# A graph network on one core: layer 0 uses six more one-hot matrices, and the attribute product is done in four 64 by 64 tiles

## The chip, the cores and the metric

The kernel runs on one core of a Trainium2 chip. The metric is device time in microseconds (us) of one execution, as the median of several. A core has TensorE (matmul into PSUM), VectorE, ScalarE, GpSimd and SyncE, which run their instructions in order and wait for each other by semaphores, and DMA engines for transfers. In the profile PE is a TensorE matmul, PEld a weight load, DVE is VectorE, ACT is ScalarE, POOL is GpSimd, SP is SyncE; SPq, ACTq and so on are their DMA queues.

## The reference

A graph has 3125 nodes with 64 features and 103125 directed edges with 64 features, sorted by their target `dst`. Each of four layers does

```
msg   = relu(h[src] + e) + 1e-7        # e = edge_attr @ enc_edge_w + enc_edge_b, the same in all layers
m     = msg * t
ex    = exp(m - max of m over the edges of dst)
agg   = sum over the edges of dst of msg * ex / sum of ex
z     = relu(layernorm((h + agg) @ w1 + b1)) @ w2 + b2
```

with `h = x @ enc_node_w + enc_node_b` at first, and layer norms and residuals between the layers. All is float32.

## The kernel before

**Streams and chunks.** The sorted edges are cut into two halves. Half 0 lies on partitions 0 to 63 and half 1, reversed, on partitions 64 to 127, one feature to a partition and one edge to a column: 51712 columns, in 49 chunks of 1024 and a tail of 512, 512, 256, 128 and 128. Each layer goes over the 54 chunks, with running maxima and sums over the columns (scans on VectorE) in place of segment operations.

**One chunk c.** TensorE makes `x = h[src] + e` in one of four PSUM buffers `X` (two banks of 512 columns each):
- `edge_product` multiplies the attributes (`attr`, 128 rows: both halves' features) by `enc_edge2`, a block-diagonal 128 by 128 matrix with `enc_edge_w` twice, one matmul to a bank (L533). It waits for the buffer: `num_ready` of chunk c-4, VectorE's last scan of it (L956).
- `add_rows` adds `h[src]`: GpSimd gathers 128 rows of the table `z_table` at a time (L492, 16 gathers for a full chunk, 8 for each half), and TensorE adds them by transposes (L562). There are three gather buffers.
- For the `CHOSEN` chunks the second bank is not gathered (8 gathers less): `add_by_one_hot` adds `h[src]` by 150 matmuls with a one-hot matrix of 3200 node rows by 2 x 512 columns (L552), split into 25 blocks by three bf16 parts of the table by two halves. A matmul has all 128 rows and 64 output columns; halves 0 and 1 go in turn to PSUM partitions 0 to 63 and 64 to 127. Pieces 0 and 1 are part 0 (60 matmuls), pieces 2 to 4 are part 1 (90).

Then ScalarE applies the relu and t (L669, L671), VectorE runs the maximum (L925) and subtracts (L930), ScalarE takes exponentials (L681 to L686), VectorE sums (L940, L943, L956) and turns the sums (L911), and SyncE stores them (L362). ScalarE also makes penalties at segment starts from `keep` bytes that SyncE loads from DRAM (L352, L659).

**The one-hot matrices.** In layer 0 VectorE builds 31 of them, for the chunks in `BANKS`: chunks 0 and 1, the even ones from 4 to 48, and 5, 13, 21, 29, 37, 45. Each has five pieces (L1020), built into the one buffer `one_hot` while VectorE does chunks c-3 (part 0) and c-2 (part 1); ScalarE prepares lanes for it (L698). SyncE stores each to DRAM, and in layers 1 to 3 ScalarE's queue loads them for all 31 chunks. In layer 0 TensorE itself uses 23 of them, those in `FIRST_CHOSEN` (even, 4 to 48). A build waits until the matrix before it is stored, and, where that one is used in layer 0, until TensorE has used the same part (`used`).

**TensorE's order** for chunk c in layer 0 is: `add_rows(c)`, `edge_product(c + 2)`, part 1 for chunk c+1, part 0 for chunk c+2. In layers 1 to 3 part 1 comes ahead of `edge_product`.

**Other work of layer 0.** Beside chunks 1 to 25 GpSimd gathers keys (L474) and ScalarE counts them, to find where each node's sums will lie. Between layers the sums are gathered for the nodes (L507) and the node network runs in seven groups.

Of the kernel before, what the change touches and what calls it, by code (L numbers as in the profile page):

```python
# [4 lines left out]
P = 128  # L5
F = 64
# [6 lines left out]
HALVES = 2  # L13
CH = 1024
KT = CH // P
BANK = 512
SLOTS = 3
XS = 4
# [7 lines left out]
NBLK = -(-COLS // CH)  # L26
TAIL = [512, 512, 256, 128, 128]
WIDTHS = [CH] * ((COLS - sum(TAIL)) // CH) + TAIL
STARTS = [sum(WIDTHS[:_c]) for _c in range(len(WIDTHS))]
NCH = len(WIDTHS)  # L30
# [22 lines left out]
PARTS = [(0, SPLIT), (SPLIT, PIECES_1H)]  # L53
HOT_SLOTS = 2
BIT_SLOTS = 3
FIRST_CHOSEN = [c for c in range(NCH) if c % 2 == 0 and 4 <= c <= 48]
CHOSEN = [c for c in range(NCH) if c < 2 or (c % 2 == 0 or c % 8 == 5) and 4 <= c <= 48]
BUILD_SLOT = {0: 50, 1: 52}
BANKS = sorted(set(FIRST_CHOSEN + CHOSEN), key=lambda c: BUILD_SLOT.get(c, c))
# [9 lines left out]
def width(c):  # L69
    return WIDTHS[c]  # L70
# [10 lines left out]
def chosen(layer):  # L81
    return FIRST_CHOSEN if layer == 0 else CHOSEN

# [27 lines left out]
def block_of(c):  # L111
    return STARTS[c] // CH, STARTS[c] % CH


def keep_chunks(b):
    return range(b * KEEP_CHUNKS, min((b + 1) * KEEP_CHUNKS, NCH))

# [10 lines left out]
def gnn_kernel(nc, x_nodes, x_t, dst_stream, src_tiles, src_banks, attr_t, enc_node_w, enc_node_b, enc_edge_w, enc_edge_b,  # L128
# [12 lines left out]
    with ExitStack() as ctx:  # L141
        def sb(name, shape, dt=f32):
            return ctx.enter_context(nc.sbuf_tensor(name, shape, dt))
# [10 lines left out]
        ident = sb("ident", [P, P])  # L154
        ones = sb("ones", [P, P])
        eps_col = sb("eps_col", [P, 1])
        enc_edge2 = sb("enc_edge2", [P, P])
        edge_bias = sb("edge_bias", [P, 1])
        enc_node = sb("enc_node", [F + 1, F])
        w1 = sb("w1", [F + 1, LAYERS, HID])  # L160
# [19 lines left out]
        attr = slots("attr", SLOTS, [P, CH])  # L180
# [64 lines left out]
        blk, five, power = (scratch[:, n * SUB:(n + 1) * SUB] for n in (3, 4, 5))  # L245
# [24 lines left out]
        X = [ctx.enter_context(nc.psum_tensor(f"X{s}", [P, CH], f32)) for s in range(XS)]  # L270
# [11 lines left out]
        x_landed, dst_landed, consts_landed, consts_set = sem("x_landed"), sem("dst_landed"), sem("consts_landed"), sem("consts_set")  # L282
# [39 lines left out]
        def _(sp):  # L322
# [7 lines left out]
            sp.dma_start(idx[:, :], src_tiles).then_inc(idx_landed, 16)  # L330
            sp.wait_ge(consts_set, 1)
            for h in range(HALVES):
                sp.dma_start(enc_edge2[h * F:(h + 1) * F, h * F:(h + 1) * F], enc_edge_w).then_inc(consts_landed, 16)
            sp.dma_start(edge_bias[:, :], enc_edge_b).then_inc(consts_landed, 16)

            def load_attr(g):
                if g >= SLOTS:
                    sp.wait_ge(attr_used, g - SLOTS + 1)
                c = g % NCH
                blk, at = block_of(c)  # L340
                sp.dma_start(attr[g % SLOTS][:, 0:width(c)], attr_t[blk * P:(blk + 1) * P, at:at + width(c)])\  # L341
                    .then_inc(attr_landed[g % SLOTS], 16)

            def load_keep(k):
# [70 lines left out]
            for layer in range(LAYERS):  # L415
                for c in range(NCH):
                    g = layer * NCH + c
# [5 lines left out]
                    if layer == 0:  # L423
                        for part in (1, 0):
                            n = bank_built_for(c + 2 + (part == 0))
                            if n is not None:
                                store_part(n, part)
                        n = bank_built_for(c + 2)
# [83 lines left out]
        def _(pe):  # L512
            pe.wait_ge(x_landed, 16 * N_X)
            pe.wait_ge(consts_set, 3)
            for i, (t0, n) in enumerate(H0_GROUPS):
                for t in range(t0, t0 + n):
                    last = nc.tensor.matmul(h0_bank[i][:, (t - t0) * F:(t - t0 + 1) * F], xT[:, t * P:(t + 1) * P],
                                            enc_node[:, :], start=True, stop=True)
# [7 lines left out]
            def edge_product(layer, c):  # L526
                g = layer * NCH + c
                s = g % SLOTS
                pe.wait_ge(attr_landed[s], 16 * (g // SLOTS + 1))
                if g >= XS:  # L530
                    pe.wait_ge(num_ready, g - XS + 1)
                for b in range(0, width(c), BANK):
                    last = nc.tensor.matmul(X[g % XS][:, b:b + BANK], enc_edge2[:, :], attr[s][:, b:b + BANK],  # L533
                                            start=True, stop=False)
                last.then_inc(attr_used, 1)

            def add_by_one_hot(layer, c, part):
# [63 lines left out]
            for layer in range(LAYERS):  # L601
# [20 lines left out]
                g = layer * NCH + NCH - 1  # L622
                w = width(NCH - 1)
# [4 lines left out]
                for n in range(2):  # L628
                    last = nc.tensor.matmul(ends_at(layer)[:, (n + 1) * P:(n + 2) * P], state[g % 2][:, n, w - 1:w], ident[:, :],
                                            start=True, stop=True)  # L630
# [613 lines left out]
```

## Time and profile before

| | us |
|---|---|
| median of 3 runs | 3443.28 |
| lowest and highest | 3441.72 and 3448.09 |
| the profiled execution | 3450.53 |
| its span, first to last instruction | 3448.7 |
| busy: PE, DVE, POOL, ACT | 2758.4, 2874.7, 2358.5, 1782.7 |
| mean granted clock of TensorE | 0.875 of 2.4 GHz |

Layer 0 ends at about 930 us of the span, layers 1, 2 and 3 run from about 1000, 1820 and 2632 us, with the node network between them. A window `A:B` of the profile is a stretch of the span. Busy time says how long an engine's instructions ran in it; the chain that ended last says what the end of the span hung on, followed back from wait to wait.

### The profile page before, as it was taken

Reading aid. Unit: us, or ns where it says so; the run is one execution under the profiler, and the core shown is the slowest. Engines: PE = TensorE matmul, PEld = TensorE weight load, DVE = VectorE, ACT = ScalarE, POOL = GpSimd, SP = SyncE. Lnnn points to the kernel's source line nnn. Section 1 sums busy time; section 2 is a strip of 40 time slices with the busy share of each in tenths; the row PEclk is TensorE's granted clock in tenths of the full one; section 3 lists DMA queues with packets and bytes.
Section 4 is the critical chain, followed back from the end, with each engine's and each line's share of the span. In section 5 each row is a group of like instructions: output and inputs, shape, how many; then the busy total and the mean of one; then the engine's idle time right before and its main releaser. Section 6 shows DMA issues by size and latency. Waiting matters only on the chain.

```text
span 3448.7 us, 51735 instructions
## 1 busy us (share of the span) xinstructions
PE 2758.4 (80%) x20152; PEld 1420.6 (41%) x20152; DVE 2874.7 (83%) x2835; ACT 1782.7 (52%) x2240; POOL 2358.5 (68%) x2429
## 2 busy tenths in 40 slices
PE   3767676777279999999758999999938999999964
PEld 2333333333144445444434444444415444444433
DVE  5899999999857888888876888888875888888895
ACT  2677775666424444555433444544443545444544
POOL 5777777777357777777627777777735777777752
PEclk7888888889679999999959999999967999999985
DMA  5999999999838999999847999999963999999971
GB/s 146 278 277 297 299 277 266 274 282 297 234 120 265 277 300 299 302 283 294 209 119 212 298 298 292 282 296 294 286 150 125 292 289 294 305 299 296 278 181 40
DMA packets 1050710, 879.63 MB, mean 255 GB/s; under 512 B 912475, under 2 KB 939616, under 8 KB 1018657
## 3 DMA queue, kind: packets, MB, share of 16 engines
q1 hardware_dynamic: 942832, 478.76, 53.8%
q10 hardware_dynamic: 28960, 305.28, 23.6%
q0 software_dynamic: 78672, 92.29, 11.0%
q8 instruction: 158, 2.59, 0.3%
q14 instruction: 88, 0.71, 0.1%
HBM read 557.36 MB, written 318.70 MB: 254 GB/s over the span
## 4 chain that ended last, share of the span: by engine, by line
DVE 29%; PE 27%; SPq 12%; POOL 11%; issue 8%; ACT 6%; DMA 6%; POOLq 0%; ACTq 0%; DVEq 0%
PE X L552 21%; POOL gath L492 10%; SPq L362 9%; DVE decay L925 6%; DVE state_all L956 5%; DMA keep<-keep_dram 5%; DVE rows_all L911 4%; PE X L533 3%; DVE one_hot L1020 3%; DVE X L930 3%; DVE state_all L940 2%; SPq L352 2%; SPq L341 1%; ACT X L671 1%; ACT msg L669 1%
## 5 line engine op out<-in xcount | busy, mean ns | idle before, releaser
L492 POOL DMA_INDIRECT gath<-z_table,idx x2296 | 2238.3, 975 | 857.3 <-issue 710.0
L552 PE MATMUL X<-one_hot,z_parts 128*64 128x512 fp8e5 x10650 | 1228.7, 392 | 111.7 <-DVE one_hot L1020 94.4
L552 PEld LDWEIGHTS X<-one_hot,z_parts 128*64 128x64 bf16 x10650 | 607.0, 113 | 759.6 <-DVE one_hot L1020 128.1
L552 PE MATMUL X<-between,z_parts 128*64 128x512 fp8e5 x6750 | 749.1, 381 | 0.0
L681 ACT ACTIVATE decay<-X 128x1024 f32<-128x1024 f32 (+2 forms) x216 | 209.1, 968 | 916.1 <-DVE X L930 893.5
L533 PE MATMUL X<-attr,enc_edge 128*128 128x512 f32 x824 | 478.6, 709 | 243.1 <-DVE state_all L956 235.8
L552 PEld LDWEIGHTS X<-between,z_parts 128*64 128x64 bf16 x6750 | 376.0, 110 | 377.5 <-issue 51.1
L911 DVE STREAM_TRANSPOSE rows_all<-state_all 128x1024 f32<-128x1024 f32 (+3 forms) x432 | 505.8, 1171 | 17.3 <-DMA rows_table<-rows_all 9.8
L940 DVE TENSOR_TENSOR_SCAN state_all<-decay,state_all,X 128x1024 f32<-128x1024 f32 (+2 forms) x216 | 468.2, 2167 | 20.0 <-ACT X L686 20.0
L925 DVE TENSOR_TENSOR_SCAN decay<-X,decay 128x1023 f32<-128x1023 f32 (+2 forms) x216 | 477.1, 2209 | 7.9 <-DVE decay L923 0.2
L956 DVE TENSOR_TENSOR_SCAN state_all<-decay,state_all,X 128x1024 f32<-128x1024 f32 (+2 forms) x216 | 467.9, 2166 | 0.0
L669 ACT ACTIVATE msg<-X,edge_bias 128x1024 f32<-128x1024 f32 (+2 forms) x216 | 226.2, 1047 | 334.8 <-PE X L562 334.7
L923 DVE TENSOR_TENSOR decay<-decay,top 128x1 f32<-128x1 f32 x216 | 33.8, 157 | 395.0 <-ACT X L671 377.3
L659 ACT ACTIVATE decay<-keep 128x1024 f32<-128x1024 uint8 (+2 forms) x216 | 213.8, 990 | 231.6 <-DMA keep<-keep_dram 231.6
L533 PEld LDWEIGHTS X<-attr,enc_edge 128*128 128x128 f32 x824 | 162.8, 221 | 414.1 <-issue 404.7
L562 PE MATMUL X<-ident,gath 128*128 128x128 f32 x1152 | 186.5, 300 | 164.9 <-DMA gath<-z_table,idx 164.9
L943 DVE SCALAR_TENSOR_TENSOR X<-msg,X 128x1024 f32<-128x1024 f32 (+2 forms) x216 | 250.5, 1160 | 7.5
L562 PEld LDWEIGHTS X<-ident,gath 128*128 128x128 f32 x1152 | 142.7, 153 | 272.6 <-DMA gath<-z_table,idx 180.4
L930 DVE TENSOR_TENSOR X<-X,decay 128x1024 f32<-128x1024 f32 (+2 forms) x216 | 249.8, 1156 | 0.0
L671 ACT ACTIVATE X<-msg,tcol 128x1024 f32<-128x1024 f32 (+2 forms) x216 | 229.6, 1063 | 7.0
L507 POOL DMA_INDIRECT between<-rows_table,pos_i x100 | 95.5, 955 | 180.9 <-DMA rows_table<-ends_row 106.7
L684 ACT ACTIVATE decay<-decay 128x1024 f32<-128x1024 f32 (+2 forms) x216 | 213.2, 987 | 0.0
(160 smaller groups left out, 1689.9 us busy)
## 6 DMA issues: line engine op xcount, KB each, us to landing
rows_table<-rows_all SPq DMA_DIRECT2D x784, 256.0 KB
attr<-attr_t SPq DMA_DIRECT2D x196, 512.0 KB
one_hot<-one_hot_dram ACTq DMA_DIRECT2D x48, 1920.0 KB
between<-one_hot_dram ACTq DMA_DIRECT2D x45, 1920.0 KB
one_hot<-one_hot_dram ACTq DMA_DIRECT2D x48, 1280.0 KB, 8.6
one_hot_dram<-one_hot SPq DMA_DIRECT2D x31, 1920.0 KB, 10.4
between<-one_hot_dram ACTq DMA_DIRECT2D x45, 1280.0 KB
one_hot_dram<-one_hot SPq DMA_DIRECT2D x31, 1280.0 KB
```

The source lines that it names most:

```text
L362: sp.dma_start(rows_by_chunk[blk, a, :, b0:b0 + n, :], rows[g % 2][a * SQ:(a + 1) * SQ, 0:n].rearrange("i b q j -> i b (q j)")).then_inc(s ...
L492: pool.indirect_dma_start(out=gath[s][:, n * F:(n + 1) * F], out_offset=None, in_=z_table, in_offset=bass.IndirectOffsetOnAxis(ap=idx[:, c ...
L533: last = nc.tensor.matmul(X[g % XS][:, b:b + BANK], enc_edge2[:, :], attr[s][:, b:b + BANK], start=True, stop=False)
L552: last = nc.tensor.matmul(x[h * F:(h + 1) * F, BANK:CH], z_parts[:, i * GB + k, third, :], bank[:, i, k, h * BANK:(h + 1) * BANK], start=F ...
L562: last = nc.tensor.matmul(X[g % XS][:, k * P:(k + 1) * P], gath[s][:, k * P:(k + 1) * P], ident[:, :], is_transpose=True, start=False, sto ...
L669: nc.scalar.activation(msg[s][:, 0:w], X[g % XS][:, 0:w], ACT.Relu, bias=edge_bias[:, :]).then_inc(msg_ready, 1)
L671: nc.scalar.activation(X[g % XS][:, 0:w], msg[s][:, 0:w], ACT.Copy, scale=tcol[:, layer:layer + 1])\
L911: v.transpose(rows[g % 2][:, 0:w // SQ, q, :], state[g % 2][:, q, 0:w].rearrange("p (b j) -> p b j", j=SQ))\
L925: v.tensor_tensor_scan(out=m[:, 1:w], data0=x[:, 0:w - 1], data1=m[:, 1:w], initial=m[:, 0:1], op0=ALU.max, op1=ALU.add).then_inc(run_max, 1)
L930: v.tensor_tensor(x, x, m, ALU.subtract).then_inc(shifted, 1)
L940: v.tensor_tensor_scan(out=state[g % 2][:, 0, 0:w], data0=decay[s][:, 0:w], data1=X[g % XS][:, 0:w], initial=state[(g - 1) % 2][:, 0, befo ...
L956: v.tensor_tensor_scan(out=state[g % 2][:, 1, 0:w], data0=decay[s][:, 0:w], data1=X[g % XS][:, 0:w], initial=state[(g - 1) % 2][:, 1, befo ...
```

## The change

In layer 0 the chunks 5, 13, 21, 29, 37 and 45 join `FIRST_CHOSEN`: their second bank is filled from the one-hot matrix in place of eight gathers and four transposes each. Builds of the matrices that follow them (6, 14, 22, 30, 38, 46) now wait for their use too.

The attribute product uses `enc_edge_w` twice one above the other (`enc_edge2` is 128 by 64), and each matmul has 64 rows and 64 output columns: bank b of half h is made from rows 64b to 64b+63 of `attr`, columns 512h to 512h+511. So a full chunk has four matmuls of 512 columns where it had two, in the order (bank, half) = (0,0), (0,1), (1,0), (1,1). The host lays the attributes out for it: rows are the bank, columns the half. A short chunk has one bank and uses 64 rows and twice the columns; its loads have 64 rows.

```diff
-FIRST_CHOSEN = [c for c in range(NCH) if c % 2 == 0 and 4 <= c <= 48]
+FIRST_CHOSEN = [c for c in range(NCH) if (c % 2 == 0 or c % 8 == 5) and 4 <= c <= 48]
...
+def attr_place(c):
+    blk, at = block_of(c)
+    if width(c) == CH:
+        return blk * P, 0, P
+    return blk * P + at * HALVES // CH * F, at * HALVES % CH, F
...
-        enc_edge2 = sb("enc_edge2", [P, P])
+        enc_edge2 = sb("enc_edge2", [P, F])
...
-                sp.dma_start(enc_edge2[h * F:(h + 1) * F, h * F:(h + 1) * F], enc_edge_w).then_inc(consts_landed, 16)
+                sp.dma_start(enc_edge2[h * F:(h + 1) * F, :], enc_edge_w).then_inc(consts_landed, 16)
...
-                blk, at = block_of(c)
-                sp.dma_start(attr[g % SLOTS][:, 0:width(c)], attr_t[blk * P:(blk + 1) * P, at:at + width(c)])\
+                row, at, parts = attr_place(c)
+                n = HALVES * min(width(c), BANK)
+                sp.dma_start(attr[g % SLOTS][0:parts, 0:n], attr_t[row:row + parts, at:at + n])\
                     .then_inc(attr_landed[g % SLOTS], 16)
...
-                for b in range(0, width(c), BANK):
-                    last = nc.tensor.matmul(X[g % XS][:, b:b + BANK], enc_edge2[:, :], attr[s][:, b:b + BANK],
-                                            start=True, stop=False)
+                w = min(width(c), BANK)
+                for b in range(-(-width(c) // BANK)):
+                    for h in range(HALVES):
+                        last = nc.tensor.matmul(X[g % XS][h * F:(h + 1) * F, b * BANK:b * BANK + w], enc_edge2[b * F:(b + 1) * F, :],
+                                                attr[s][b * F:(b + 1) * F, h * w:(h + 1) * w], start=True, stop=False)
                 last.then_inc(attr_used, 1)
```

The host's part of the diff (how `attr_s` is filled, block by block, after `attr_place`) is left out.

## Rows read from the trace of the kernel before

**Rows 1.** The page's groups: count, busy us, mean ns, idle before.
```profile
L533 PE MATMUL X<-attr,enc_edge 128*128 128x512 f32 x824 | 478.6, 709 | 243.1 <-DVE state_all L956 235.8
```

**Rows 2.** The view by stretches, all engines; behind them clock, DMA share, GB/s.
```profile
650.00:750.00 100.00, 75.71 (x509) 36.17 (x510) 99.16 (x75) 66.97 (x67) 77.44 (x75) 0.85 1.00 291
1200.00:1400.00 200.00, 185.70 (x1443) 92.44 (x1440) 167.59 (x127) 99.41 (x100) 147.88 (x157) 0.97 1.01 297
```

**Rows 3.** The chain that ended last, by line: layer 0 to 500 us.
```profile
by line: POOL gath L492 68.8%; issue 21.6%; POOL between L474 5.0%; DMA gath<-z_table,idx 2.8%; PE X L562 0.7%; DVE decay L925 0.6%; ACT X L671 0.3%; ACT msg L669 0.3%; POOLq L465 0.2%; DVE decay L923 0.0%
```

**Rows 4.** The same chain from 500 to 930 us.
```profile
by line: DVE one_hot L1020 25.9%; DVE decay L925 13.9%; issue 9.9%; DVE X L930 7.3%; DVE state_all L956 6.3%; DVE state_all L940 6.0%; ACT x_sb L698 5.8%; ACT between L698 4.4%; DVE rows_all L911 3.6%; ACT decay L681 3.3%; ACT X L686 3.3%; 
```

**Rows 5.** The same chain in layers 1, 2 and 3, one after another.
```profile
by line: PE X L552 39.7%; SPq L362 12.9%; PE X L533 6.7%; DVE decay L925 6.2%; DVE state_all L956 6.0%; issue 4.5%; DVE rows_all L911 4.2%; DMA keep<-keep_dram 3.7%; DVE X L930 3.2%; DVE state_all L940 2.5%; SPq L341 2.0%; PE X L562 2.0%; A
...
by line: PE X L552 28.8%; SPq L362 14.8%; DMA keep<-keep_dram 10.4%; DVE decay L925 6.5%; DVE state_all L956 6.4%; issue 5.4%; DVE rows_all L911 4.8%; PE X L533 4.7%; SPq L352 4.3%; DVE X L930 3.4%; DVE state_all L940 2.2%; SPq L341 2.1%; A
...
by line: PE X L552 28.2%; SPq L362 11.7%; DMA keep<-keep_dram 8.2%; DVE decay L925 7.6%; DVE state_all L956 7.4%; issue 5.7%; DVE rows_all L911 5.6%; SPq L352 4.9%; PE X L533 4.3%; DVE X L930 4.0%; DVE state_all L940 2.9%; SPq L341 2.3%; AC
```

**Rows 6.** Stretches again, VectorE alone, in layer 0's first half.
```profile
188.00:250.00 62.00, 56.36 (x42) 0.86 0.96 276
250.00:350.00 100.00, 93.62 (x71) 0.86 1.00 301
350.00:450.00 100.00, 92.99 (x70) 0.84 0.99 297
450.00:495.00 45.00, 43.33 (x33) 0.82 0.98 272
```

**Rows 7.** GpSimd's gathers in the same part: stretch, busy us, count.
```profile
196.00:490.00 294.00, 212.41 (x203) 0.85 0.99 290
```

**Rows 8.** Pieces of the chain in layer 0: start us, us, what.
```profile
553.65 7.09 DVE one_hot L1020 x5
...
684.56 7.09 DVE one_hot L1020 x5
703.56 4.29 DVE one_hot L1020 x3
```

**Rows 9.** TensorE's instructions in time, layer 1: start us, us, what, idle before.
```profile
1394.67 3.75 PE L533 MATMUL X<-attr,enc_edge 128*128 128x512 f32 x4 [6.29 <-DVE state_all L956]
...
1406.80 9.90 PE L552 MATMUL X<-between,z_parts 128*64 128x512 fp8e5 x90
...
1418.55 6.67 PE L552 MATMUL X<-one_hot,z_parts 128*64 128x512 fp8e5 x60
1425.14 0.66 PE L562 MATMUL X<-ident,gath 128*128 128x128 f32 x4
```

**Rows 10.** Pieces of the chain there.
```profile
1394.67 3.75 PE X L533 x4
...
1416.70 1.91 PE X L533 x4
...
1507.79 3.75 PE X L533 x4
```

**Rows 11.** TensorE's weight loads at one cold and one warm attribute product.
```profile
1395.66 0.33 PEld L533 LDWEIGHTS X<-attr,enc_edge 128*128 128x128 f32 x1 [0.52 <-issue]
1396.51 0.33 PEld L533 LDWEIGHTS X<-attr,enc_edge 128*128 128x128 f32 x1 [0.52 <-issue]
...
1417.17 0.19 PEld L533 LDWEIGHTS X<-attr,enc_edge 128*128 128x128 f32 x1 [0.24 <-issue]
1417.60 0.19 PEld L533 LDWEIGHTS X<-attr,enc_edge 128*128 128x128 f32 x1 [0.24 <-issue]
```

**Rows 12.** Who waited for whom in layer 1's steady part: us, times, longest.
```profile
POOL gath L492 <- PE X L562: 13.7, 13, 2.2
```

**Rows 13.** GpSimd's gathers in time in that part.
```profile
1398.06 0.94 POOL L492 DMA_INDIRECT gath<-z_table,idx  x1 [0.30 <-issue]
1399.31 0.94 POOL L492 DMA_INDIRECT gath<-z_table,idx  x1 [0.30 <-issue]
```

More of the change, by code:

```diff
@@ L1206 @@
     src_b = np.stack([streams(src, 0)[:, c * CH + BANK:(c + 1) * CH] for c in BANKS]).reshape(P, SUB)
-    attr_s = chunked(streams(attr, 0)).transpose(1, 0, 3, 2).reshape(NBLK * P, CH)
+    attr_h = streams(attr, 0)
+    attr_s = np.zeros((NBLK * P, CH), attr.dtype)
+    for c in range(NCH):
+        row, at, parts = attr_place(c)
+        w = min(width(c), BANK)
+        for b in range(parts // F):
+            for h in range(HALVES):
+                attr_s[row + b * F:row + (b + 1) * F, at + h * w:at + (h + 1) * w] = \
+                    attr_h[h, STARTS[c] + b * BANK:STARTS[c] + b * BANK + w].T
     nxt = list(range(1, LAYERS)) + [0]
```

## The prediction

> **What bounds the kernel now.** I read the costliest groups first, where the product to be changed has 824 records [rows 1], then the stretches [rows 2], then the chain that ended last stage by stage [rows 3 to 5], since the share of busy time is an average over stages with different limits. The reader is to see three limits. In layer 0 up to about 500 us the chain is GpSimd's gathers and their issue gaps, 90% of it [rows 3], while VectorE is 93% busy and not waited for [rows 6]. From there to the end of layer 0 VectorE is 99% busy [rows 2] and the chain is its work: building the one-hot matrices and the scans [rows 4]. In layers 1 to 3 no engine stands alone. TensorE is busy for 93% of a stretch, its clock is 0.97, the DMA engines are at 1.01 [rows 2], and the chain changes between TensorE's one-hot products, SyncE's stores, the keep loads and VectorE [rows 5].
>
> **Part 1: layer 0 uses six more matrices.** The matrices of chunks 5, 13, 21, 29, 37 and 45 are built, stored and paid for already; only the use in layer 0 is new. Removed: the gathers of the last four tiles of both halves, 8 per chunk, 48 in all, and 24 of TensorE's transposes. Added: 6 x 150 one-hot matmuls, and a wait of the next build for the matrix to be used.
>
> What the gathers are worth: between 196 and 490 us GpSimd issues 203 gathers and some 14 key gathers in 294 us [rows 7], 1.355 us each. Chunks 5, 13 and 21 lie in the stage that they bound: 24 x 1.355 = 32.5 us off GpSimd's path. But VectorE is next. In the four stretches from 188 to 495 us it is idle 5.6 + 6.4 + 7.0 + 1.7 = 20.7 us [rows 6], and where it is the bound it still idles 0.8% [rows 2], here some 2.6 us. So at most 18 us can be won. Some of the idle time falls before a gather is spared, and the last gather of a chunk still has to land, so I take 14, with 5 and 18 as ends. The gathers of chunks 29, 37 and 45 lie beside VectorE's 99% and give nothing: if that cover were gone they would be 32 us more.
>
> What the 900 matmuls cost: 90 of them take 9.90 us and 60 take 6.67 us, with the tail of the pipeline [rows 9], so 16.5 us a chunk and 99 us in all, beside VectorE. TensorE's cover is thinnest at a run of three chosen chunks (12, 13, 14). Eight of VectorE's chunks with five builds take 684.56 - 553.65 = 130.9 us, a build of five pieces 7.1 [rows 8]; that leaves (130.9 - 35.5) / 8 = 11.9 us for a chunk without a build, and 19.0 with a whole one, as 703.56 - 684.56 shows. TensorE's is 0.6 (transposes) + 1.9 (attribute product) + 9.8 + 6.6 = 18.9 us [rows 9, 10]. It fits, just. The build of part 0 of the next matrix waits until part 0 of this one is used. TensorE may start part 1 of the matrix before it 2.8 us ahead of VectorE's chunk (two pieces), so it has used both after -2.8 + 9.8 + 6.6 = 13.6 us; VectorE comes to that build after 11.9 + 4.3 = 16.2: 2.6 us to spare. Behind that build on VectorE's queue stands the next chunk's running maximum, and behind the transposes stands ScalarE's message. A run of three costs 0 to 1 us if the product stays below 2.4 us. Six runs, half of them in the VectorE stage: 2 us. Part 1 is then -12 us, from -18 to -3.
>
> **Part 2: the attribute product in four tiles.** Before, a chunk has two matmuls of 128 rows by 512 columns against a block-diagonal matrix; the trace shows four records, each with a weight load [rows 9, 11]. So an f32 matmul is two passes, one after another in program order. A pass starts 0.43 us after the one before it at the full clock (1417.17 to 1417.60) and 0.85 us at the half clock (1395.66 to 1396.51) [rows 11]; 2.4 and 1.2 GHz. The product takes 1.91 us warm, 4 x 0.43 + 0.19, and 3.75 us cold, 4 x 0.85 + 0.35 [rows 10]. After it, a chunk has four matmuls, eight passes of the same 512 columns. Their price isn't in the trace. It hangs on how many run beside one another.
> - Nothing overlaps: 8 passes, 3.63 us warm and 7.15 us cold.
> - Each tile runs by itself, all four together: 2 passes, 1.05 and 2.05 us.
> - Passes start in program order, and one to a busy tile holds up those behind it. Then the second pass of a tile waits for its first, and the first pass of the next tile can start only beside that second pass. Three overlaps of eight: 5 passes, 2.34 and 4.60 us, so +0.43 warm and +0.85 cold.
>
> The nearest rows are the one-hot products. There consecutive matmuls go to column tiles 0 and 1 in turn, and 60 take 6.67 us [rows 9], 0.22 us a pair, which is one stream of 512 columns at the full clock. So two tiles do overlap when consecutive instructions go to different tiles. No row shows two consecutive ones to one tile overtaken by a third. I take 5 passes: it is what those rows give with the passes in program order, and keep 2 and 8 for the range. The Trainium skill (TensorE: Matmul & The Clock Gate, "The mechanism") says that matmuls start and end strictly in program order; by that rule the sum is the one with 5 passes. Its page TensorEngine Tiling (Array Packing), "Theoretical Speedup", promises up to 2x for each small dimension; by that the product would be the one with 2 passes. The trace of before can't tell these two apart, for its pairs are single passes.
>
> What that costs in layers 1 to 3: the product's share of the chain is 6.7% of 745, 4.7% of 740 and 4.3% of 728 us [rows 5], 116 us. In the chain that is 12 cold products, 36 warm ones (pieces like those of [rows 10]) and four cut pieces. At 5 passes: 12 x 0.85 + 36 x 0.43 = 26 us more. But a sixth to a quarter of the chain there is SyncE's row stores and the landing of keep loads [rows 5], which are slow because the DMA engines are full [rows 2], and slower work asks for less a microsecond. So up to half may be absorbed: 13 to 26, I take 19. Paths that now lie just beside the chain could bring it to 35. In layer 0 the product is on no chain [rows 3, 4], beyond the 2 us above. The changed weights' memset is shorter and loads keep their bytes; the short chunks' 64-row loads come at a layer's end, two chunks ahead: nothing.
>
> **The sum.** -12 + 19 = +7 us. The profiled execution took 3450.5 us (span 3448.7); with the change 3457.5. The median of the runs shown lies 7.2 us under it, so about 3450. Own range: -18 + 8 to -3 + 35, so 3433 to 3475. A measurement of this kernel can tell about 0.2% (7 us) from no change, so this case is on the edge of "same" and "slower".
>
> **The rivals.**
> - Four tiles side by side, 2 passes. For it: the pairs do overlap [rows 9]. Against it: a pass to a busy tile would have to be passed over. The chain would lose 12 x 1.70 + 36 x 0.86 = 51 us. GpSimd caps this: eight chunks have 3 x 16 + 5 x 8 = 88 gathers, one each 1399.31 - 1398.06 = 1.25 us [rows 13], 110 us in a period of 1507.79 - 1394.67 = 113 us [rows 10], so 3 us a period, and its waits for TensorE in layer 1 are only 13.7 us [rows 12]. That leaves 20 to 48, I take 30. With 14 from layer 0: 3399. It is the likeliest way to faster, and is decided where the product falls under 1.7 us.
> - A wash: the tiles overlap so far that the product costs about 4 passes. Only part 1 counts, with little lost: 3431.
> - No overlap, 8 passes. For it: all of the trace's f32 matmuls run singly. Against it: the one-hot pairs. 12 x 3.4 + 36 x 1.72 = 103 us on the chain, some absorbed, less 5 from layer 0, where runs of three chosen chunks now overrun VectorE's period by 1.6 us: 3533. It decides for slower from a product above 2.4 us.
>
> **How the numbers follow.** Chances: 5 passes 0.45, 2 passes 0.25, a wash 0.15, 8 passes 0.15. Range 3388 to 3490: it leaves out the last case, the tails of the first and the far part of the second. Faster by over 0.2%: 0.25 + 0.13 + 0.04 = 0.42; same 0.20; slower 0.15 + 0.23 = 0.38.
>
> **What would show it.** Part 1: up to 500 us the chain turns from GpSimd to VectorE, which goes from 93% to 97% busy, and the chunks after chunk 25 begin some 14 us earlier; right if layer 0 ends by 5 to 18 us sooner. TensorE's idle time in 650 to 750 us shrinks, and no wait of VectorE's build for a one-hot product exceeds 1 us. Part 2: the group of the attribute product has 1648 records (eight for each of 49 full chunks and four for each of five short ones, in four layers); the stretch of one product warm is 2.3 us (5 passes), 1.1 (2) or 3.6 (8), and cold twice that; this one duration decides between the cases. The 8-chunk period of layer 1, 113 us, becomes 114 to 115, or 110. The prediction is wrong if the passes of one tile are overtaken, or if full DMA queues, and not TensorE, set layers 1 to 3, so that 2 or 5 passes make no difference there.

## The result, and the profile after

The changed kernel takes 3426.2 us (median of 5, 3417.0 to 3427.1) against 3443.3 us: ratio 0.9945, interval 0.993 to 0.9959. Measured once more beside the kernel before, on another chip, it took 3429.5 against 3442.6 us: 0.9964, 0.9952 to 0.9977. So it is faster by 13 to 17 us, 0.4 to 0.5%, where the forecast was 7 us slower. The profiled execution took 3417.0 us, its span 3415.2. Single executions scatter by about 10 us to either side, so the 33.5 us between the two spans overstate the gain.

Two groups of the page (those of the attribute product answer to [rows 1]):

```profile
L500 POOL DMA_INDIRECT gath<-z_table,idx x2248 | 2193.5, 976 | 861.8 <-issue 691.1
...
L543 PE MATMUL X<-attr,enc_edge 64*64 64x512 f32 (+1 forms) x1648 | 270.0, 706 | 309.6 <-DVE state_all L966 300.2
```

The attribute product has its 1648 records, but it keeps TensorE busy for 270.0 us in place of 478.6. There are 48 gathers less.

Stretches, with all engines (answering to [rows 2]), then VectorE alone in layer 0 (answering to [rows 6]):

```profile
650.00:750.00 100.00, 83.12 (x669) 39.57 (x665) 99.16 (x75) 64.06 (x64) 66.98 (x64) 0.90 0.99 285
1200.00:1400.00 200.00, 180.78 (x1556) 88.40 (x1554) 172.31 (x131) 101.10 (x102) 151.35 (x160) 0.95 1.01 296
```

```profile
188.00:250.00 62.00, 58.94 (x44) 0.83 0.98 273
250.00:350.00 100.00, 96.59 (x73) 0.92 1.01 311
350.00:450.00 100.00, 96.59 (x73) 0.93 0.99 303
```

In layer 0 VectorE is now idle for 3.1 + 3.4 + 3.4 us in stretches where it was idle for 5.6 + 6.4 + 7.0. In 650 to 750 us it is 99.16% busy as before, though TensorE's busy time rose from 75.7 to 83.1 us. In layer 1 TensorE went from 92.9% to 90.4% and its granted clock from 0.97 to 0.95. The DMA share stays at 1.01.

The chain by line, from 100 to 500 us (answering to [rows 3]) and in layer 1 (answering to [rows 5]; the bounds of the window are the same, though layer 1 starts 12 us sooner):

```profile
by line: DVE one_hot L1030 15.2%; DVE decay L935 11.8%; issue 11.4%; PE X L562 8.2%; DVE X L940 6.2%; DVE state_all L950 5.2%; DVE state_all L966 5.0%; ACT x_sb L708 4.7%; ACT between L708 3.9%; DMA one_hot_dram<-one_hot 3.0%; ACT decay L69
```

```profile
by line: PE X L562 19.5%; SPq L370 13.7%; POOL gath L500 10.8%; DMA keep<-keep_dram 8.6%; issue 7.9%; SPq L360 7.2%; DVE decay L935 5.7%; DVE state_all L966 5.6%; DVE rows_all L921 4.8%; DVE X L940 2.9%; ACT X L681 2.0%; ACT msg L679 2.0%; 
```

GpSimd's gathers had 69% of the first stretch and are gone from its head; VectorE's builds and scans stand there. In layer 1 the product (PE X, L533 before, L543 now) is no longer among the large entries, where it had 6.7%. In its place are SyncE's issue of keep loads (L360), the landing of them, and GpSimd's gathers.

Pieces of the chain in layer 0 (answering to [rows 8]): the build that ran at 553.65 us runs at 541.83, the one at 665.57 in the trace of before at 653.83. Layer 0 is 11.8 us ahead at both, and keeps that to its end.

```profile
541.83 7.09 DVE one_hot L1030 x5
...
653.83 7.09 DVE one_hot L1030 x5
```

TensorE in layer 1, a cold product with the one-hot matmuls behind it and a warm one (answering to [rows 9, 10]):

```profile
1378.94 1.99 PE L543 MATMUL X<-attr,enc_edge 64*64 64x512 f32 x8 [3.28 <-DVE state_all L966]
1380.85 8.49 PE L562 MATMUL X<-between,z_parts 128*64 128x512 fp8e5 x60
...
1400.13 1.09 PE L543 MATMUL X<-attr,enc_edge 64*64 64x512 f32 x8
1401.15 6.67 PE L562 MATMUL X<-one_hot,z_parts 128*64 128x512 fp8e5 x60
```

A warm product takes 1401.15 - 1400.13 = 1.02 us where it took 1.91, a cold one 1380.85 - 1378.94 = 1.91 where it took 3.75. That is two passes and their start, the price of the first rival, and not five.

### The profile page after: what moved, and what is told of

Read it like the earlier page. It is cut to its first block, busy times and chain, and to the rows that moved or that the text cites. A ratio compares the mean times of both kernels' runs of the same rounds, so it can differ in the third digit from the quotient of the medians.

```text
span 3415.2 us, 55099 instructions
## 1 busy us (share of the span) xinstructions
PE 2701.8 (79%) x21852; PEld 1362.3 (40%) x21852; DVE 2874.3 (84%) x2835; ACT 1783.1 (52%) x2240; POOL 2315.3 (68%) x2381
## 4 chain that ended last, share of the span: by engine, by line
DVE 33%; PE 17%; SPq 15%; ACT 9%; DMA 9%; issue 9%; POOL 8%; DVEq 0%; ACTq 0%; POOLq 0%
PE X L562 14%; SPq L370 9%; POOL gath L500 8%; DVE decay L935 7%; DMA keep<-keep_dram 7%; DVE state_all L966 5%; DVE one_hot L1030 5%; SPq L360 5%; DVE rows_all L921 4%; DVE X L940 4%; DVE state_all L950 2%; ACT X L681 2%; ACT msg L679 2%; SPq L349 1%; ACT x_sb L708 1%
## 5 line engine op out<-in xcount | busy, mean ns | idle before, releaser
L500 POOL DMA_INDIRECT gath<-z_table,idx x2248 | 2193.5, 976 | 861.8 <-issue 691.1
L562 PE MATMUL X<-one_hot,z_parts 128*64 128x512 fp8e5 x11550 | 1356.4, 397 | 148.5 <-DVE one_hot L1030 124.8
L562 PEld LDWEIGHTS X<-one_hot,z_parts 128*64 128x64 bf16 x11550 | 667.9, 115 | 874.2 <-DVE one_hot L1030 163.1
L562 PE MATMUL X<-between,z_parts 128*64 128x512 fp8e5 x6750 | 764.2, 386 | 0.0
L543 PE MATMUL X<-attr,enc_edge 64*64 64x512 f32 (+1 forms) x1648 | 270.0, 706 | 309.6 <-DVE state_all L966 300.2
L692 ACT ACTIVATE X<-X 128x1024 f32<-128x1024 f32 (+2 forms) x216 | 208.1, 963 | 0.0
L696 ACT ACTIVATE X<-X 128x1024 f32<-128x1024 f32 (+2 forms) x216 | 207.1, 959 | 0.0
```

The source lines that it names most:

```text
L500: pool.indirect_dma_start(out=gath[s][:, n * F:(n + 1) * F], out_offset=None, in_=z_table, in_offset=bass.IndirectOffsetOnAxis(ap=idx[:, c ...
L543: last = nc.tensor.matmul(X[g % XS][h * F:(h + 1) * F, b * BANK:b * BANK + w], enc_edge2[b * F:(b + 1) * F, :], attr[s][b * F:(b + 1) * F, ...
L562: last = nc.tensor.matmul(x[h * F:(h + 1) * F, BANK:CH], z_parts[:, i * GB + k, third, :], bank[:, i, k, h * BANK:(h + 1) * BANK], start=F ...
```

## The experiments

The kernels ran on five chips, on each of them beside the kernel before. Two of the chips behave differently (told below); the times in the table are from the three on which the kernel before took 3440 to 3443 us, so two kernels from different chips are compared to some 3 us. The first two rows are from one chip, the next four from another, the last two from a third.

| kernel | us | ratio to before (interval) |
|---|---|---|
| matrices only | 3432.4 | 0.9977 (0.9961 to 0.9993) |
| four tiles only | 3440.8 | 0.9991 (0.9979 to 1.0004) |
| changed kernel, again | 3429.5 | 0.9964 (0.9952 to 0.9977) |
| changed, three keep buffers | 3400.8 | 0.9882 (0.9866 to 0.9899) |
| changed, fewer gathers | 3413.3 | 0.9921 (0.9902 to 0.9939) |
| matrices only, fewer gathers | 3430.5 | 0.9961 (0.9946 to 0.9975) |
| changed, three keep buffers, fewer gathers | 3350.7 | 0.9738 (0.9718 to 0.9757) |
| matrices only, three keep buffers | 3409.0 | 0.9915 (0.9897 to 0.9934) |

### Each part alone

Matrices only is the kernel before with one line changed:

```diff
-FIRST_CHOSEN = [c for c in range(NCH) if c % 2 == 0 and 4 <= c <= 48]
+FIRST_CHOSEN = [c for c in range(NCH) if (c % 2 == 0 or c % 8 == 5) and 4 <= c <= 48]
```

> Part 1 alone: layer 0 uses the six more matrices, the attribute product stays one block-diagonal matmul to a bank. Theory A (the two parts add up: GpSimd hands layer 0 over to VectorE, whatever the product costs): layer 0 ends 10 to 12 us sooner, as in the changed kernel (last scan at 925.1 against 936.7 us), layers 1 to 3 keep their lengths, about 3432 us, ratio 0.997. Rival B (the gain of layer 0 needs the shorter product, for a run of three chosen chunks takes TensorE 18.9 us a chunk beside VectorE's 19.0): layer 0 ends only 3 to 8 us sooner and VectorE shows idle time of 1 us and more ahead of builds or running maxima around chunks 6, 14, 22, ...: 3437 us or more.

Four tiles only is the changed kernel with that line turned back.

> Part 2 alone: the product in four tiles, layer 0 uses 23 matrices as before. Theory A: layer 0 stays as it was, since GpSimd and then VectorE bound it (last scan at 936 to 937 us); layers 1 to 3 are shorter by 2 to 10 us each, as far as GpSimd's 1.25 us a gather lets them: 3443 - 7 to 3443 - 22, so 3421 to 3436. Rival C (full DMA engines set layers 1 to 3, and their shortening in the one profile of the changed kernel is scatter): no change, 3440 to 3446.

Measured: 9.6 us faster for the matrices, 1.3 us for the tiles, which is no difference that can be told. The product of the two ratios is 0.9968; the changed kernel has 0.9964 and 0.9945. The parts add up within the scatter: beside the matrices the tiles are worth 2 to 8 us (13 to 17 less 9.6 to 11).

For layers 1 to 3 theory A failed: it gave the tiles 7 to 22 us there. The number is rival C's, no change. Its reason, full DMA engines, does not stand: with a third keep buffer the same layers get shorter though the DMA share stays (below).

The traces are sharper than the times. From the start of VectorE's running maximum of chunk 5 to that of chunk 28 (L925, one scan to a chunk) the kernel before takes 408.3 us and four tiles only 408.8. Matrices only takes 397.6, the changed kernel 397.1, twice. From chunk 28 to the last scan of layer 0 all four take 375.8 to 376.1. So the 11 us come from the matrices, in the part that GpSimd bounded, and do not depend on the product. For layer 0 theory A holds.

Rival B is right in a small thing. Ahead of chunk 5 matrices only loses up to 4 us, since the run of chunks 4, 5 and 6 is TensorE's there. Pieces of the chain, matrices only first, then the changed kernel:

```profile
114.31 3.41 PE X L533 x4
117.72 16.53 PE X L552 x144
...
134.84 1.72 PE X L533 x4
```

```profile
112.44 1.92 PE X L543 x8
114.36 16.56 PE X L562 x150
...
131.50 1.02 PE X L543 x8
```

The two products stand on the chain at the start of this run: 3.41 + 1.72 us in blocks, 1.92 + 1.02 us in tiles. Chunk 5's maximum starts at 156.0 us there, at 151.9 here. In two other profiles with the block-diagonal product and the matrices it starts at 155.4 and 152.5, so this loss comes and goes. One of VectorE's builds waits 1.5 us for a one-hot product in matrices only; in the changed kernel none does.

### Does a busy tile hold up the others

The prediction hung on this. Both kernels cut each 512-column matmul of the product into two of 256 columns (`u`). One issues them back to back to the same tile, the other goes round the tiles:

```diff
                 for b in range(-(-width(c) // BANK)):
                     for h in range(HALVES):
-                        last = nc.tensor.matmul(X[g % XS][h * F:(h + 1) * F, b * BANK:b * BANK + w], enc_edge2[b * F:(b + 1) * F, :],
-                                                attr[s][b * F:(b + 1) * F, h * w:(h + 1) * w], start=True, stop=False)
+                        for u in range(2):
+                            last = nc.tensor.matmul(X[g % XS][h * F:(h + 1) * F, b * BANK + u * q:b * BANK + (u + 1) * q],
+                                                    enc_edge2[b * F:(b + 1) * F, :],
+                                                    attr[s][b * F:(b + 1) * F, h * w + u * q:h * w + (u + 1) * q],
+                                                    start=u == 0, stop=False)
```

This is the same tile twice in a row; the other kernel has the loop over `u` outermost. `q` is `w // 2`.

> The changed kernel with each 512-column matmul of the attribute product cut into two of 256 columns, issued one behind the other to the same tile (tile 0, tile 0, tile 1, tile 1, ...). Theory P (a pass to a busy tile does not hold up those behind it for other tiles): the product still takes as long as one tile's own work, about 1.0 us warm as now. Theory Q (TensorE takes matmuls in program order, and only the two passes within one f32 matmul are no obstacle): the second matmul of a tile holds up the next tile until the first is through, five steps of 0.43 us, about 2.3 us warm. The whole kernel by P 3420 us, by Q slower than the one before by some 10 us.

> The same cut into 256 columns, issued tile by tile in turn (four tiles, then the four again): the control for the kernel that issues the same tile twice in a row. Both theories: about 1.0 us warm for a product, unless sixteen passes in place of eight cost by themselves, which this shows.

TensorE in time at a warm product, same tile first, and then tiles in turn:

```profile
1406.04 1.11 PE L545 MATMUL X<-attr,enc_edge 64*64 64x256 f32 x16
1407.09 6.67 PE L566 MATMUL X<-one_hot,z_parts 128*64 128x512 fp8e5 x60
```

```profile
1402.15 1.10 PE L545 MATMUL X<-attr,enc_edge 64*64 64x256 f32 x16
1403.18 6.67 PE L566 MATMUL X<-one_hot,z_parts 128*64 128x512 fp8e5 x60
```

1407.09 - 1406.04 = 1.05 us against 1403.18 - 1402.15 = 1.03. By theory Q the first would have been 2.3. Nor is this one product alone. The group of all products on the two pages, same tile first and then tiles in turn, keeps TensorE busy for nearly the same time:

```profile
L545 PE MATMUL X<-attr,enc_edge 64*64 64x256 f32 (+1 forms) x3296 | 279.6, 445 | 337.6 <-DVE state_all L970 327.9
L545 PE MATMUL X<-attr,enc_edge 64*64 64x256 f32 (+1 forms) x3296 | 271.9, 440 | 317.1 <-DVE state_all L970 308.6
```

A pass to a busy tile holds nobody up: theory P. Two matmuls, four passes, for the same tile stand ahead of the next tile's in the kernel, and the product is no longer for it.

The whole times, one execution each, were 3444.2 us for the same tile first (P had said 3420, Q some 10 us over the kernel before, so some 3452) and 3428.7 us for the tiles in turn. Their layers 0 take 872.3 and 873.5 us, so the difference lies in layers 1 to 3, where the product is as long in both. The first lies outside the 3417 to 3436 us that the changed kernel showed; why is open. The theories are decided by the product's own time alone.

The same is seen in the changed kernel itself. Its weight loads at the product of 1400.13 us, and then TensorE's matmuls in flight (the number in brackets) in three short stretches behind it:

```profile
1400.13 0.21 PEld L543 LDWEIGHTS X<-attr,enc_edge 64*64 64x64 f32 x8 [0.41 <-issue]
```

```profile
1400.30:1400.40 0.10, 0.10 (x4) 1.00 1.56 632
1400.50:1400.60 0.10, 0.10 (x4) 1.00 0.90 317
1400.66:1400.76 0.10, 0.10 (x8) 1.00 0.66 251
```

All eight weight loads begin and end within 0.21 us, so both passes' weights are in before the first pass is through. The profile models the ends of matmuls, and does not name their tiles. At 0.2 and 0.4 us four passes are in flight, as I read it one to a tile; at 0.55 us the records of the first four overlap those of the second four. If each matmul's two passes held up the rest, one pass would have been in flight at 0.4 us.

### Where the tiles' time went

In four tiles only the product's group takes 282.2 us of TensorE in place of 478.6, 196 us less, and the kernel's time is the same. Part of it went to the one-hot matmuls. Their two groups on the page, in the kernel before and in four tiles only:

```profile
L552 PE MATMUL X<-one_hot,z_parts 128*64 128x512 fp8e5 x10650 | 1228.7, 392 | 111.7 <-DVE one_hot L1020 94.4
L552 PE MATMUL X<-between,z_parts 128*64 128x512 fp8e5 x6750 | 749.1, 381 | 0.0
```

```profile
L562 PE MATMUL X<-one_hot,z_parts 128*64 128x512 fp8e5 x10650 | 1253.4, 397 | 141.0 <-DVE one_hot L1030 114.5
L562 PE MATMUL X<-between,z_parts 128*64 128x512 fp8e5 x6750 | 770.2, 389 | 1.1 <-DMA between<-one_hot_dram 1.1
```

The same 17400 matmuls take 2023.6 us in place of 1977.8, 46 us more, and the mean granted clock of the run fell from 0.875 to 0.857. The rest became waiting. Waits in layers 1 to 3 (1040 to 3300 us), before and after the whole change:

```profile
ACT decay L659 <- DMA keep<-keep_dram: 225.1, 61, 8.0
...
PE X L533 <- DVE state_all L956: 173.0, 41, 10.5
```

```profile
ACT decay L669 <- DMA keep<-keep_dram: 239.8, 67, 9.1
...
PE X L543 <- DVE state_all L966: 232.5, 42, 10.3
```

ScalarE waits for keep loads 240 us in all (225 before), and TensorE's wait for a free PSUM buffer (VectorE's last scan) grew from 173 to 232 us. The test gives the keep bytes a third buffer, so that each load is issued one pair of chunks sooner:

```diff
-KEEP_SLOTS = 2
+KEEP_SLOTS = 3
...
-                    if c % KEEP_CHUNKS == 0 and c < NCH - KEEP_CHUNKS and layer * NKEEP + c // KEEP_CHUNKS >= 1:
+                    if c % KEEP_CHUNKS == 0 and c < NCH - KEEP_CHUNKS * (KEEP_SLOTS - 1) and layer * NKEEP + c // KEEP_CHUNKS >= 1:
...
-                    load_keep((layer + 1) * NKEEP)
+                    for j in range(KEEP_SLOTS - 1):
+                        load_keep((layer + 1) * NKEEP + j)
```

> Three keep buffers, on a chip as the first. Theory G (GpSimd's gathers set layers 1 to 3): within 4 us of the changed kernel. Rival K (the keep loads took the gain of the shorter product): ScalarE's waits for keep under 100 us in place of 240, and 10 to 30 us shorter.

3400.8 us, 28.7 less than the changed kernel on the same chip. Its profile has no wait for a keep load among the 60 longest from 1040 to 3300 us. Rival K's numbers came out, and theory G, that the gathers alone set layers 1 to 3, falls. K's reason, that the keep loads took the gain of the shorter product, holds in small part only: the same buffer takes the kernel with matrices only, whose product is long, from 3432.4 to 3409.0 us (another chip). So 23 of the 29 us could be had without the tiles. The chain of the changed kernel with three buffers in layer 1:

```profile
by line: POOL gath L501 50.0%; PE X L563 19.7%; issue 19.0%; DMA gath<-z_table,idx 1.8%; DVE decay L936 1.7%; DVE state_all L967 1.6%; DVE state_all L951 1.3%; PE X L573 1.3%; PE X L544 1.3%; DVE X L941 0.9%; DVE rows_all L922 0.9%; ACT X L
```

Now 69% of it is GpSimd's gathers and issue gaps. So GpSimd is the limit right behind the keep loads.

### Behind them: GpSimd

Fewer gathers: in layers 1 to 3 a full chunk without a one-hot matrix has 14 gathers in place of 16; the last tile of both halves keeps what was in the buffer, and the sums are made of that.

```diff
+def fetched_tiles(layer, c):
+    return gathered_tiles(layer, c) - (layer > 0 and gathered_tiles(layer, c) == KT)
...
-                    for n in range(first_tile(c) * HALVES, gathered_tiles(layer, c) * HALVES):
+                    for n in range(first_tile(c) * HALVES, fetched_tiles(layer, c) * HALVES):
```

> 14 gathers in place of 16 for the full chunks without a one-hot matrix in layers 1 to 3 (the last tile of both halves stays as it was in the buffer), product in four tiles. Theory G: 80 to 140 us shorter than the changed kernel, about 3320 us; a period of eight chunks 102 to 106 us. Rival F (full DMA engines): 0 to 15 us shorter, 3412 us or more.

> The same cut of gathers with the block-diagonal product and the six more matrices in layer 0. Theory G: TensorE is the next bound, a period of 108 us or more, 20 to 60 us behind the kernel with tiles and fewer gathers. Rival F: within 5 us of the kernel with matrices only, 3430 us.

With tiles 3413.3 us, 16 less than the changed kernel on the same chip; with the block-diagonal product 3430.5, 2 less than matrices only on its own chip (some 5 by the ratios). Theory G's 80 to 140 us failed. Both numbers are rival F's, but not F's reason: full DMA engines would leave nothing for the tiles, and here they are worth 17 us on one chip. The chain in layer 1, in matrices only and in the kernel with blocks and fewer gathers:

```profile
by line: PE X L552 40.6%; SPq L362 12.3%; PE X L533 6.9%; DVE decay L925 6.4%; DVE state_all L956 5.8%; issue 4.5%; DVE rows_all L911 3.9%; DMA keep<-keep_dram 3.5%; DVE X L930 3.3%; SPq L341 3.0%; DVE state_all L940 2.3%; PE X L562 2.0%; A
...
by line: PE X L556 36.3%; SPq L366 11.8%; DVE decay L929 6.7%; DVE state_all L960 6.1%; DMA keep<-keep_dram 6.0%; PE X L537 6.0%; DVE rows_all L915 4.8%; issue 4.7%; DVE X L934 3.5%; SPq L356 2.7%; SPq L345 2.5%; ACT X L675 2.1%; ACT msg L6
```

TensorE's one-hot matmuls and product have 47.5% of the first and 42% of the second, and GpSimd's gathers are among the large entries of neither. With the long product TensorE has the most of the chain already, and sparing gathers brings next to nothing. In the changed kernel the gathers had 10.8% of layer 1's chain, and sparing some pays. That the one comes from the other is my reading of the chains.

Both cuts together:

> As before on a chip like the first, work left out as before (the last tile's gathers of the full chunks without a one-hot matrix in layers 1 to 3). Two limits one behind the other: 50 to 110 us less than with three buffers alone (3401), 3290 to 3350 us. Full DMA engines as the last limit: 3391 us or more.

3350.7 us, 50 less than with three keep buffers alone (another chip; 0.9738 against 0.9882). That is just at the near end of the range of two limits one behind the other, 3290 to 3350, and 40 us under the least that full DMA engines would allow. A stretch of it:

```profile
1200.00:1400.00 200.00, 184.68 (x1576) 89.93 (x1572) 180.09 (x137) 104.44 (x106) 143.41 (x152) 0.95 1.03 302
```

The DMA share was 1.01 in the changed kernel and is 1.03 here, in layers that are some 20 us shorter each: a share of 1.0 did not mean that transfers set the time. VectorE is at 90%, so no more than some 10% is left in this stretch behind it (an estimate).

### The tiles without keep waits

> Three keep buffers, block-diagonal product, six more matrices, on a chip like the first. Tiles pay once the keep waits are gone: 3413 to 3430 us. GpSimd hides the product again: 3396 to 3406 us.

3409.0 us with blocks (0.9915) against 3400.8 with tiles on another chip (0.9882): 8 us, or 11 by the ratios. It lies between the two theories. A stretch of each, tiles first:

```profile
1400.00:1600.00 200.00, 185.08 (x1588) 89.83 (x1584) 171.36 (x130) 102.13 (x103) 151.33 (x160) 0.96 1.02 301
...
1400.00:1600.00 200.00, 189.27 (x1499) 95.57 (x1496) 168.64 (x128) 101.79 (x104) 150.98 (x161) 0.99 1.01 297
```

GpSimd makes 160 and 161 gathers in 200 us, as many with the long product as with the short one, so it hides the product for the most part; TensorE goes from 93% to 95% busy.

What the tiles are worth is then 1 us alone, 2 to 8 us beside the matrices, 8 to 11 with a third keep buffer and 17 with fewer gathers. With both of these together it was not measured, so how much of the 51 us that the prediction's first rival counted on the chain would come through is open.

### On other chips

On two chips the kernel before took 4731 and 4597 us. A stretch of layer 1 of the changed kernel on the first of them, and its chain in layer 1:

```profile
1400.00:1800.00 400.00, 291.21 (x2019) 130.92 (x2016) 234.62 (x176) 138.34 (x138) 206.64 (x220) 0.82 0.75 203
...
by line: PE X L562 59.5%; issue 24.9%; PE X L543 5.9%; PE X L572 4.6%; SPq L370 1.4%; DVE state_all L966 0.8%; DVE decay L935 0.7%; DVE rows_all L921 0.6%; DVE X L940 0.3%; DVE state_all L950 0.3%; DMA keep<-keep_dram 0.2%; ACT X L681 0.1%;
```

Here 203 GB/s are moved where the case's chips move 296 in layer 1, with the DMA engines busy for 0.75 and VectorE for 59%. The chain is TensorE's one-hot matmuls and issue gaps, time in which the engine waits for nothing that the profile shows; the keep loads have 0.2% of it and GpSimd's gathers are not among its large entries. What makes these chips slow is not shown. The ratios say little of this case. They are told because they show how far the verdicts travel.

> The changed kernel unaltered, beside this call's other kernels, for a closer ratio and a second profile. Theory A (part 1 gives 11 us in layer 0, part 2 next to nothing in layers 1 to 3, since GpSimd already runs at 98 to 99% of one gather each 1.25 us there): 3428 to 3432 us. Rival D (the two parts help each other: a product that is short and matrices used in layer 0): 3422 to 3426 us.

0.9972 (0.9952 to 0.9991): the change pays there too, 0.3%. It was repeated on a chip as the first:

> The changed kernel once more: in the last call the chip moved some 200 GB/s where the first two moved 300, and both kernels took over 4700 us, so its four runs tell little of this case. On a chip as the first, by theory A 3428 to 3432 us, by rival D 3422 to 3426 us.

That gave the 3429.5 us of the table, theory A's.

> The changed kernel with three buffers for the keep bytes in place of two, so that each load is issued one pair of chunks sooner. Theory G (GpSimd's gathers set layers 1 to 3, and the waits for keep loads lie beside them): same as the changed kernel, within 4 us. Rival K (the keep loads behind SyncE's stores, 7 to 14% of the chain of the changed kernel, took the gain of the shorter product): ScalarE's waits for keep fall from 240 us to under 100, and layers 1 to 3 are 10 to 30 us shorter.

0.9965: the third keep buffer brings nothing beyond the change, where it brought 0.8% on the case's chips. So this chip gives theory G's number and the case's chips give rival K's.

> The changed kernel with 14 gathers in place of 16 for the full chunks of layers 1 to 3 that use no one-hot matrix; the last tile of both halves is left as it was in the buffer, its transposes stay. Theory G: a period of eight chunks falls from 111 us towards the next bound, at the least (88 - 6) x 1.25 = 102 us, so 5 to 8 us less in each, some 18 periods: 80 to 140 us shorter, about 3320 us. Rival F (the full DMA engines, at a share of 1.01, set the period; this saves only 0.2 of 33 MB in it): 0 to 15 us shorter, 3412 us or more.

> The same cut of gathers with the attribute product as before (block-diagonal, two matmuls), and the six more matrices in layer 0. Theory G: TensorE, at 104 to 107 us of work in a period, is the next bound: 108 us or more, so at least 3 us a period behind the kernel with tiles and fewer gathers, 20 to 60 us in all: the four tiles pay once GpSimd lets go. Rival F: as with tiles, within 5 us of the kernel with matrices only.

0.9705 and 0.9786. The cut takes 126 us off the changed kernel on this chip (4721.4 to 4595.1), as theory G had it, and with blocks the kernel is 32 us behind that with tiles (0.8%), in G's 20 to 60 too. GpSimd has no large entry in the chain here, so why fewer gathers count for so much is open.

> The changed kernel with three keep buffers and 14 gathers in place of 16 for the full chunks without a one-hot matrix in layers 1 to 3 (the last tile of both halves stays as it was in the buffer). If keep loads and GpSimd are two limits one behind the other: the eight-chunk period falls from 110 to between 102 and 107 us, 50 to 110 us less than with three buffers alone, 3290 to 3350 us. If the full DMA engines are the last limit: within 10 us of 3401 us.

0.979, 4501.7 us on the second of these chips. The times forecast are those of the case's chips; the two theories were decided there, above.

> Three keep buffers with the block-diagonal product and the six more matrices. If the tiles pay once the keep waits are gone: 12 to 30 us slower than the same with tiles (3401), so 3413 to 3430 us. If GpSimd hides the product again: within 5 us of 3401 us.

1.0044, 4619.2 us.

> Three keep buffers and three more one-hot chunks (9, 25, 41) in all layers. Layer 0 builds three more matrices, 3 x 7.1 = 21 us slower. In layers 1 to 3, if GpSimd is what is left: 9 x 8 x 1.25 = 90 us of gathers gone, TensorE and VectorE then let 30 to 60 of it through, so 3360 to 3390 us. If the DMA engines are full for real (3.3 MB more for each, 11 us at 300 GB/s): 3420 us or more.

1.0111, 4646.3 us. Its edit is `or c % 16 == 9` in both lists of chunks. The changed kernel with three keep buffers and no more matrices was not run on this chip, so what the three matrices cost by themselves is not shown. Whether they pay at 300 GB/s was not tried.

> The kernel before with three keep buffers and nothing else. If the keep loads were the first limit already: 10 to 20 us faster than before, 3425 to 3433 us. If TensorE's longer product was the first limit and the keep waits only took its place in the changed kernel: within 5 us of 3442 us.

0.9996, 4596.8 us: the second theory's number, on this chip. On the case's chips this kernel was not run; the nearest there is matrices only with three keep buffers, 23 us under matrices only.

The kernel with blocks and three keep buffers differs from this one by the six matrices alone, and takes 22 us more. From the running maximum of chunk 28 to the last scan of layer 0 it takes 440.8 us against 417.1. So part 1, which gains 10 us on the case's chips, loses 22 on this one, at least beside three keep buffers. Why is open.

## Why the prediction was wrong

**Part 1 was right.** -12 us was forecast, from 18 to 3. The layer's last scan ends its path 11.6 us sooner by the traces (it starts at 925.1 in place of 936.7 us), and 9.6 us were timed for the part alone. It came as argued: GpSimd hands over to VectorE after 11 of the 32.5 us that the spared gathers are worth (14 were put down). The VectorE stage behind chunk 28 did not lose the 2 us put down for the runs of three: it takes 376 us with and without the matrices, with either product.

**The step that failed** is "I take 5 passes: it is what those rows give with the passes in program order". The product takes two passes' time, 1.02 us warm. The term that was built on it, +19 us for layers 1 to 3, measured -1.3 us in four tiles only. What was wrong is the assumption that a pass to a busy tile holds up those behind it; the same-tile kernel shows that it does not, for two matmuls in a row. The one-hot rows could not have decided it, since there every matmul goes to the other tile. The Trainium skill's rule is that matmuls start strictly in program order (TensorE: Matmul & The Clock Gate, "The mechanism"). The trace does not agree with what the prediction made of it: four passes are in flight 0.2 us after the start, and the product takes 1.02 us, not 2.3. Whether TensorE overtakes, or the program interleaves the passes ahead of it, these runs tell apart only so far: with two matmuls to a tile written back to back, the product still took 1.05 us. The Trainium skill's table of speedups (TensorEngine Tiling (Array Packing), "Theoretical Speedup") gives up to 2x for a small dimension. The trace agrees: from 1.91 to 1.02 us the product is 1.9 times as fast.

**With the failed step mended, the sum would have been wrong on the other side.** The rival with two passes said 3399 us; it is 3426 to 3430. Its 30 us for layers 1 to 3 were 1.3 us for the tiles alone, and some 2 to 8 together with the matrices (13 to 17 less 9.6 to 11). Three things stood between:
- A cold product was to save 1.70 us. It did save 1.84 by itself, but the matmuls behind it gave part back. TensorE in the kernel before, the one-hot matmuls behind the cold product at 1394.67:

```profile
1398.35 7.49 PE L552 MATMUL X<-between,z_parts 128*64 128x512 fp8e5 x60
```

They took 7.49 us there and take 8.49 now, behind a shorter product: the granted clock is 0.50 in both products, and 0.88 in the matmuls behind the first and 0.78 in those behind the second. Of 1.84 us 1.0 went back at this place. Over the whole run with four tiles only it was 46 of 196 us, and the prediction had no term for it.
- The next wait was named wrongly. GpSimd's 1.25 us a gather was taken as the cap. It is one of two limits, and the smaller: the third keep buffer, which leaves the gathers alone, won 28.7 us, fewer gathers alone 16, both together 79. The keep loads stood in the chain before with 3.7% to 10.4% [rows 5], and were only used as a discount on the slower case. The chance that full DMA queues and not TensorE set layers 1 to 3 stood as the last sentence of the prediction, without a price; the 79 us, won at a DMA share of 1.03, speak against it.
- Much of the rest of TensorE's time came back as waiting for a PSUM buffer, 59 us more of it.

**The sign** was the sum of a right -12 and a wrong +19. The range, 3388 to 3490, held the time, and the wash (3431, part 1 only) came nearest of the cases. That was luck: the product did not cost four passes, it cost two, and the time it saved was lost to waits.

## What to carry to other kernels

Where several engines are at 90% and more, a shorter step on one of them moves the time only as far as the next limit, here a few us; ask for each wait in the chain, the transfers' too, what it would take to remove it. The cheapest limit to lift in this kernel was a buffer of 2 KB a partition: the third keep buffer took 28.7 us off the changed kernel, about twice what the change gave, and 23 us off the kernel with the long product. And where an unknown overlap decides the sign, measure it alone: the time of one product would have done.

## What the runs showed of the hardware

- Four 64 by 64 tiles of TensorE work on f32 side by side: eight passes of 512 columns in 1.02 us, where four passes over the whole array took 1.91. Sixteen passes of 256 columns take 1.03 and 1.05 us, whether the tiles come in turn or the same tile twice in a row.
- A shorter step at the half clock can leave more of what follows at the half clock: 1.84 us saved on one product, 1.0 given back by the 60 matmuls behind it, whose granted clock was 0.78 in place of 0.88; over the run 196 us saved and 46 given back, with the mean granted clock at 0.857 in place of 0.875.
- A DMA share of 1.0 did not mean that transfers were the limit: at 1.01 the changed kernel takes 3429.5 us, and without keep waits and with 108 gathers fewer it takes 3350.7, at 1.03.
- The same kernel takes 3440 to 3443 us on some chips and 4597 to 4731 on others, where some 200 GB/s are moved in place of 300. A third keep buffer is worth 0.8% on the first and nothing on the others, and the six matrices gain 10 us on the first and lose 22 on one of the others (there with three keep buffers).
